# A transformer block and a gated cross-attention: all sixteen heads' probabilities turned by VectorE in 23 of 48 items, with a second exchange through DRAM issued from ScalarE's queue

## The chip, the cores and the metric

One core of one Trainium2 chip. The metric is the device time of one execution in microseconds, the median of three runs. Matrix products run on TensorE (PE), the rest on VectorE (DVE), ScalarE (ACT) and GpSimd (POOL); SyncE (SP) only issues DMAs.

## The reference, cut to what matters

```python
def attention(q, k, v, mask):                       # 16 heads of 32
    scores = einsum('bhqd,bhkd->bhqk', q, k) / sqrt(32)
    scores = scores * mask - 10000.0 * (1.0 - mask)
    return einsum('bhqk,bhkd->bhqd', softmax(scores), v)
# x: (16, 128, 512), enc: (16, 128, 512), float32
y = layernorm(x) @ w_qkv + b_qkv;  x = x + attention(q, k, v of y, mask_a) @ w_ao + b_ao
q = layernorm(x) @ w_q + b_q; k, v = enc @ w_kv + b_kv
x = x + attention(q, k, v, mask_b) @ w_co + b_co
x = x + gelu(layernorm(x) @ w1 + b1) @ w2 + b2
a = layernorm(enc); Q = x @ Wq.T; K, V = a @ Wk.T, a @ Wv.T
out = x + tanh(gate) * (softmax(Q K.T * scale, masked) V) @ Wo.T
```

## The kernel before, in words

There are three attention phases of 16 batch elements (128 tokens each): A (self attention), B (cross attention), then a feed-forward stage, then D (the gated cross attention). An *item* g is one batch element of one phase: g = 0 to 15 in A, 16 to 31 in B, 32 to 47 in D. Every product with a weight is made of three matmuls, hi·hi, hi·lo and lo·hi, of a rounded "hi" part and its remainder "lo" of each float32 operand. Projections are cut in *half units* of 512 PSUM columns per partition, three for each step (`units[0]`, `units[1]`, `units[2]`).

Each engine runs an instruction stream that is written out by hand, and steps of the five streams meet only at semaphores. Step g holds parts of three items:

- **TensorE** (`step`): `times_v(g-2)`, `scores(g)`, the projection of unit 0, `row_sums(g-1)` (a small transpose of the inverse row sums), `transpose_prob(g-1, 2)` and `(g-1, 3)` (four 128x128 transposes each, heads 8 to 15), unit 1, unit 2, `project_out(g-2)`; then the next step's `times_v(g-1)`.
- **ScalarE** (`step`): `context_hi(g-2)`, the copy of the transposed row sums (`row_sums_out`), the copy of unit 0, the copy of the transposed probabilities (`probs_out`, L1194), a weight chunk's hi part, the copy of unit 1, in some steps `fill_scale` or `fill_hi` (the layer norm's scale and bias, or the hi part, on the next pair's inputs), then 16 exponentials (`exps`, L1217; four heads are a quarter).
- **VectorE** (`step`): `context(g-2)` (the division by the row sums), in D the first half of `mask_scores(g)`, `inverse_sums(g-1)` (L1611, after all exponentials of g-1), `context_lo(g-2)` twice (L1633), `mask_scores(g)` (L1590), `row_max(g)` (L1603), in some steps `turn_inputs` (L1535), statistics and hi parts, `turn_blocks(g)` (L1617), and the residual.
- **GpSimd** (`step`): in A and B `add_mask_bias(g)` twice (L2023), between VectorE's masking and its maximum; lo parts of inputs and weights; a bias row on the residual.
- **SyncE** (`step`): all DMAs, in a fixed order.

The probabilities must be turned (keys on partitions) before `times_v`. In the items of `BY_PE` (0, 27 to 32, 44 to 47) TensorE transposes all sixteen heads. In the 37 others it transposes heads 8 to 15, and heads 0 to 7 go another way: the exponentials write them into `prob_blocks`, VectorE turns the 32x32 blocks (`turn_blocks`, one instruction), SP stores the 512 KB tile to DRAM (`store_blocks`, L516) and brings it back with four DMAs of 128 KB, one for each group of 32 partitions, with the blocks in their places (`bring_blocks`, L525). `times_v(g)` waits for the copies by ScalarE and for all four DMAs (`s_moved`). PSUM banks 4 and 5 (`T_BANK`) hold the transposes and the result of `times_v`, banks 6 and 7 (`U_BANK`) the units and the row sums.

Phase A's steps 4, 6, 8, 10 and 14 contain a `fill_scale`, step 13 a `fill_hi` of inputs that need no turning. In D the odd steps to 43 contain a `fill_scale`, the even ones to 44 a `fill_hi`, both after `turn_inputs`.

Of the kernel before, what the change touches and what calls it, by code (L numbers as in the profile page):

```python
# [152 lines left out]

def moved_number(g):

    return g + 1 - sum(k <= g for k in BY_PE)


def transposed_count(g, c):

    return sum(4 if k in BY_PE else 2 for k in range(g)) + (c + 1 if g in BY_PE else c - 1)


def copied_by_act(g, half):

    return sum(2 if k in BY_PE else 1 for k in range(g)) + (half + 1 if g in BY_PE else 1)
# [75 lines left out]
def build(nc, x, first_x, enc, encT, mask_a, mask_b, mask_d, weights, columns, rows, gate, ident_in, out):  # L242
# [3 lines left out]
    with ExitStack() as ctx:  # L246
# [18 lines left out]
        hidden_parts = sb("hidden_parts", [128, 2, 512], f32r)  # L265
        chi = [ctx_parts[:, 0, :], hidden_parts[:, 0, :]]
# [30 lines left out]
        turned = nc.dram_tensor("prob_turned", (2, 128, NH // 2 * T), f32, kind="Internal").ap()  # L297
        spread = nc.dram_tensor("row_sums_spread", (4, KC * T), f32, kind="Internal").ap()
# [20 lines left out]
        s_moved = sem("prob_blocks_moved")  # L319

# [41 lines left out]
        s_turned = sem("prob_blocks_turned")  # L362
        s_clo = sem("ctx_lo")
# [26 lines left out]
        def row_sum_bank(g):  # L390
            return U_BANK if sums_late(g) else U_BANK + 1
# [316 lines left out]
        def pe_program():  # L708
# [105 lines left out]

            def times_v(g):

                phase, q, gp, half = g // 16, (g % 16) // 2, (g // 2) % 2, g % 2
                pe.wait_ge(s_pta, copied_by_act(g, 1))
                if g in BY_PE:
                    pe.wait_ge(s_ptd, copied_by_dve(g, 1))  # L820
                else:
                    pe.wait_ge(s_moved, 64 * moved_number(g))
                if phase == D:
                    pe.wait_ge(s_va, 2 * q + half + 1)
                else:
                    pe.wait_ge(s_v, 16 * phase + 2 * q + half + 1)
                for c in range(KC):
                    for j in range(4):
                        h = 4 * c + j
                        out = ps[32 * j:32 * j + 32, T_BANK + c // 2, T * c:T * c + T]  # L830
                        P = prob[:, g % 2, T * h:T * h + T]
                        if h < NH // 2 and g not in BY_PE:
                            P = by_head(prob[:, g % 2, 0:NH // 2 * T])[:, h]
# [121 lines left out]
            def step(i, st):  # L955
# [19 lines left out]
                if st.prev:  # L975
                    row_sums(g - 1)
                    if g - 1 in BY_PE:
                        transpose_prob(g - 1, 0)
                        transpose_prob(g - 1, 1)
                    else:  # L980
                        transpose_prob(g - 1, 2)
                        if g != 44:
                            transpose_prob(g - 1, 3)
                if not late:
                    if st.prev:
                        row_sums_out(g - 1)
                    project(*st.units[1], U_BANK + 1)
                if g == 44:
                    transpose_prob(g - 1, 3)
# [158 lines left out]
        def act_program():  # L1148
# [53 lines left out]
            def exps(g, quarter, part=None):  # L1202
# [7 lines left out]
                if moved and quarter == 0 and moved_number(g) > 1:  # L1210
                    act.wait_ge(s_pst, 16 * (moved_number(g) - 1))
                for s in range(4 * quarter + (2 if part == 1 else 0), 4 * quarter + (2 if part == 0 else 4)):
                    src = P[:, T * s:T * s + T]
                    dst = src
                    if moved:
                        dst, src = by_head(pblocks[:, :])[:, s], src.rearrange("p (j k) -> p j k", k=32)
# [93 lines left out]
            def step(st):  # L1310
# [25 lines left out]
                if g == 44:  # L1336
# [9 lines left out]
                if not st.ends:  # L1346
                    half_out(*st.units[2])
                if g != 28:
# [157 lines left out]
        def dve_program():  # L1506
# [111 lines left out]

            def prob_out(g, c):
# [88 lines left out]
            def step(st):  # L1708
# [20 lines left out]
                if late:  # L1729
# [254 lines left out]
        def pool_program():  # L1984
# [30 lines left out]

            def add_mask_bias(g, h):
# [170 lines left out]
```

## Time and profile before

| | |
|---|---|
| median of 3 runs | 1102.0 us (1101.92 to 1104.04) |
| profiled execution, span from first to last instruction | 1100.7 us |
| its own time beyond the span | not recorded; 1.3 us lie between the span and the median |
| steps 3 to 14 (71.9 to 250.0 us) | 178.1 us, 12 steps |
| steps 34 to 44 (894.5 to 1053.9 us) | 159.4 us, 11 steps |

A step is counted here from the start of its `scores` (L776) to the start of the next step's. The engines' busy shares say who works; which of them bounds a step is seen from who waits last in it.

### The profile page before, as it was taken

What the parts mean: (1) busy time and instruction counts of PE and PEld (TensorE: products, weight loads), DVE (VectorE), ACT (ScalarE), POOL (GpSimd) and SP (SyncE); (2) the same over time, 40 slices, a digit from 0 to 9 for tenths busy, and PEclk for the clock granted to TensorE, in tenths of its full rate; (3) what the DMA queues carried; (4) which work ended last, traced back from release to release, by engine and by line L of the source; (5) the groups of instructions that cost most, each with busy time, mean ns of one, the idle gap of its engine ahead of it and who ended that gap; (6) DMA issues with size and microseconds to landing.
All of it is one profiled execution on the core that took longest, in us unless ns stands there. A gap on an engine that the chain in (4) does not pass through costs nothing.

```text
span 1100.7 us, 24328 instructions
## 1 busy us (share of the span) xinstructions
PE 1074.7 (98%) x8829; PEld 934.2 (85%) x8829; DVE 815.4 (74%) x1314; ACT 712.7 (65%) x2365; POOL 462.0 (42%) x337
## 2 busy tenths in 40 slices
PE   7989999999999999998999999999999999999998
PEld 6888888888888888886898888888888988888886
DVE  6678787778888778888877557656677478778777
ACT  4678777777788778786444434434444387777776
POOL 3665666557767776767512121103012331122100
PEclk9999999999999999999999999999999999999999
DMA  6366565576776777553241130220622146666633
GB/s 216 98 201 198 191 195 188 174 227 216 221 227 215 223 211 229 180 191 128 85 134 40 38 96 12 85 96 1 181 101 83 59 146 205 203 198 210 177 97 97
DMA packets 136135, 167.04 MB, mean 152 GB/s; under 512 B 16992, under 2 KB 82256, under 8 KB 136016
## 3 DMA queue, kind: packets, MB, share of 16 engines
q1 hardware_dynamic: 136016, 165.50, 47.9%
q8 instruction: 70, 1.15, 0.4%
q14 instruction: 49, 0.40, 0.1%
HBM read 113.15 MB, written 52.29 MB: 150 GB/s over the span
## 4 chain that ended last, share of the span: by engine, by line
PE 59%; DVE 12%; ACT 9%; POOL 7%; issue 4%; DMA 3%; SPq 1%; DVEq 0%; ACTq 0%; POOLq 0%
PE psum L938 15%; PE psum L919 14%; PE psum L758 13%; POOL prob L2023 6%; PE psum L858 5%; PE psum L750 5%; ACT prob L1217 4%; ACT prob_blocks L1217 2%; PE psum L794 2%; PE psum L776 2%; DVE prob L1590 2%; DVE ln_tile L1528 2%; PE psum L835 2%; DVE negmax L1603 2%; ACT inputs_transposed L1255 2%
## 5 line engine op out<-in xcount | busy, mean ns | idle before, releaser
L758 PE MATMUL psum<-inputs_hi,weights_hi 128*128 128x256 f32 x768 | 223.7, 291 | 5.4 <-POOL inputs_lo L2014 2.5
L758 PE MATMUL psum<-inputs_lo,weights_hi 128*128 128x256 f32 x768 | 217.1, 283 | 0.0
L758 PE MATMUL psum<-inputs_hi,weights_lo 128*128 128x256 f32 x768 | 217.0, 283 | 0.0
L2014 POOL TENSOR_TENSOR inputs_lo<-inputs_transposed,inputs_hi 128x512 fp32r<-128x512 f32 x84 | 113.0, 1367 | 228.9 <-DVE inputs_hi L1563 168.4
L2023 POOL TENSOR_TENSOR prob<-prob,mask_bias 128x1024 f32<-128x1024 f32 x64 | 152.7, 2408 | 98.3 <-DVE prob L1590 96.3
L1217 ACT ACTIVATE prob<-prob,negmax 128x128 f32<-128x128 f32 x472 | 182.2, 391 | 0.5 <-DVE negmax L1603 0.5
L758 PEld LDWEIGHTS psum<-inputs_hi,weights_hi 128*128 128x128 f32 x768 | 146.7, 191 | 10.3 <-issue 2.8
L1603 DVE TENSOR_REDUCE negmax<-prob 128x8 f32<-128x1024 f32 x96 | 115.9, 1210 | 50.0 <-POOL prob L2023 50.0
L758 PEld LDWEIGHTS psum<-inputs_lo,weights_hi 128*128 128x128 f32 x768 | 147.0, 191 | 0.2
L758 PEld LDWEIGHTS psum<-inputs_hi,weights_lo 128*128 128x128 f32 x768 | 146.9, 191 | 0.0
L858 PE MATMUL psum<-weights_hi,context_parts 128*128 128x512 f32 x376 | 125.8, 393 | 0.4 <-ACT kT L1168 0.3
L1217 ACT ACTIVATE prob_blocks<-prob,negmax 128x128 f32<-128x128 f32 x296 | 114.4, 389 | 16.9 <-DVE negmax L1603 16.9
L1303 ACT ACTIVATE qT<-psum,columns 128x512 f32<-128x512 f32 (+1 forms) x80 | 46.2, 598 | 106.2 <-PE psum L919 106.2
L1687 DVE SCALAR_TENSOR_TENSOR kT<-kT,qT 128x512 f32<-128x512 f32 x64 | 46.9, 733 | 80.3 <-ACT kT L1308 80.2
L2026 POOL TENSOR_TENSOR residual<-residual,bias_rows 128x512 f32<-128x512 f32 x42 | 57.7, 1378 | 83.3 <-DMA residual<-stream 63.3
L1217 ACT ACTIVATION_READ_ACCUMULATOR prob<-prob,negmax 128x1 f32 x472 | 90.3, 191 | 0.0
L938 PE MATMUL psum<-weights_hi,hidden_parts 128*128 128x512 f32 x264 | 87.7, 392 | 1.1 <-DVE hidden_parts L1682 1.0
L1255 ACT ACTIVATE inputs_transposed<-inputs_transposed,columns 128x256 f32<-128x256 f32 x120 | 62.3, 591 | 37.2 <-DVE inputs_transposed L1535 37.0
L1989 POOL TENSOR_TENSOR weights_lo<-weights_whole,weights_hi 128x512 fp32r<-128x512 f32 x56 | 75.8, 1367 | 21.3 <-ACT weights_hi L1154 21.3
L858 PEld LDWEIGHTS psum<-weights_hi,context_parts 128*128 128x128 f32 x376 | 70.6, 188 | 16.5 <-ACT qT L1303 0.6
L938 PE MATMUL psum<-weights_hi,context_parts 128*128 128x512 f32 x248 | 81.8, 390 | 0.9 <-DVE context_parts L1682 0.9
L1590 DVE SCALAR_TENSOR_TENSOR prob<-psum,mask 128x512 f32<-128x512 f32 x128 | 79.2, 680 | 0.0
(124 smaller groups left out, 2600.3 us busy)
## 6 DMA issues: line engine op xcount, KB each, us to landing
prob_turned<-prob_blocks SPq DMA_DIRECT2D x37, 512.0 KB, 3.0
prob<-prob_turned SPq DMA_DIRECT2D x148, 128.0 KB, 3.3
weights_whole<-weights_in SPq DMA_DIRECT2D x72, 256.0 KB, 3.4
normalised<-ln_tile SPq DMA_DIRECT2D x30, 512.0 KB, 2.8
inputs_transposed<-normalised SPq DMA_DIRECT2D x120, 128.0 KB, 2.9
context<-row_sums_spread SPq DMA_DIRECT2D x188, 64.0 KB, 2.1
stream<-residual SPq DMA_DIRECT2D x42, 256.0 KB, 2.7
residual<-stream SPq DMA_DIRECT2D x42, 256.0 KB, 3.7
```

What stands on the lines that cost most here:

```text
L758: mm = pe.matmul(ps[:, bank, GT * part:GT * part + GT], w[:, slot, c, o], a[:, buf, c, :], start=c == 0 and i == 0, stop=c == KC - 1 and i ...
L858: mm = pe.matmul(ps[:, U_BANK + 1, :], a[0][:, cs], w[:, slot, c, :], start=c == 0 and i == 0, stop=c == KC - 1 and i == 2)
L919: mm = pe.matmul(out, w[:, slot, c, o], a, start=c == 0 and i == 0, stop=c == KC - 1 and i == 2)
L938: mm = pe.matmul(ps[:, accumulator(group, t), :], a[gb][:, tok], w[:, slot, (j * chunks + e) % 4, :], start=j == 0 and e == 0 and i == 0, ...
L1217: ins = act.activation(dst, src, ACT.Exp, bias=negmax[:, par, s:s + 1], accum_out=total[:, par, s:s + 1])
L1255: ins = act.activation(dst, src, ACT.Identity, bias=cols[:, b0 + c:b0 + c + 1], scale=cols[:, g0 + c:g0 + c + 1])
L1590: ins = dve.scalar_tensor_tensor(heads(P[:, 512 * c:512 * c + 512]), ps[:, S_BANK:S_BANK + 4, T * c:T * c + T], SCALE, other.unsqueeze(1). ...
L1603: dve.tensor_reduce(negmax[:, par, 8 * h:8 * h + 8], heads(prob[:, par, 1024 * h:1024 * h + 1024]), AX.X, ALU.max, negate=True).then_inc(s ...
L1989: pool.tensor_tensor(wlo[:, slot, c, :], raw[:, slot, c, :], whi[:, slot, c, :].bitcast(f32), ALU.subtract).then_inc(s_wlo, 1)
L2014: pool.tensor_tensor(lo, y, hi.bitcast(f32), ALU.subtract).then_inc(s_rlo if fill.ln is None else s_flo, 1)
L2023: pool.tensor_tensor(half, half, mb.unsqueeze(1).to_broadcast([128, 8, T]), ALU.add).then_inc(s_biased, 1)
L2026: pool.tensor_tensor(tile, tile, brow[:, ROW_SLOT[name], :], ALU.add).then_inc(s_resb, 1)
```

## The change

Items 2 to 13 and 33 to 43 (`WHOLE`, 23 items) have none of their heads transposed by TensorE. Heads 8 to 15 are written by the exponentials into a new tile, `second_prob_blocks`, turned by a second VectorE instruction right after `inverse_sums(g-1)` in the next step, stored and brought back by one and four DMAs that ScalarE's stream issues: the store after the copy of unit 0, the four loads right before the next exponentials. The eight transposes and ScalarE's copy of 1024 columns go. `times_v` waits for the second exchange (`s_moved2`) and for the row sums' copy. The row sums of these items go to bank 5, after `context(g-1)`, and unit 1 then waits for the residual of g-3 and no longer for that copy. For items 1 to 13 and 32 to 43 the two `context_lo` move from VectorE to GpSimd, at the head of its step.

```diff
+WHOLE = tuple((*range(2, 14), *range(33, 44)))
+LO_BY_POOL = tuple((*range(1, 14), *range(32, 44)))
...
         def row_sum_bank(g):
-            return U_BANK if sums_late(g) else U_BANK + 1
+            return T_BANK + 1 if g in WHOLE else U_BANK if sums_late(g) else U_BANK + 1
...
# TensorE
             def row_sums(g):
                 pe.wait_ge(s_rt, g + 1)
-                if sums_late(g):
+                if g in WHOLE:
+                    pe.wait_ge(s_cx, 2 * g)
+                elif sums_late(g):
...
             def times_v(g):
-                pe.wait_ge(s_pta, copied_by_act(g, 1))
+                if g in WHOLE:
+                    pe.wait_ge(s_rc, g + 1)
+                    pe.wait_ge(s_moved2, 64 * second_number(g))
+                else:
+                    pe.wait_ge(s_pta, copied_by_act(g, 1))
...
-                    else:
+                    elif g - 1 not in WHOLE:
                         transpose_prob(g - 1, 2)
                         if g != 44:
                             transpose_prob(g - 1, 3)
                 if not late:
-                    if st.prev:
+                    if g - 1 in WHOLE:
+                        u_bank_free(g)
+                    elif st.prev:
                         row_sums_out(g - 1)
                     project(*st.units[1], U_BANK + 1)
...
# ScalarE
+            def store_second_blocks(g):
+                n = second_number(g)
+                act.wait_ge(s_turned2, n)
+                if n > 2:
+                    act.wait_ge(s_moved2, 64 * (n - 2))
+                act.dma_start(turned_second[n % 2], second_blocks[:, :]).then_inc(s_pst2, 16)
+
+            def bring_second_blocks(g):
+                n = second_number(g)
+                act.wait_ge(s_pst2, 16 * n)
+                blocks = turned_second[n % 2].rearrange("(i k) (j n) -> j k i n", i=4, j=4)
+                for j in range(4):
+                    dst = prob[32 * j:32 * j + 32, g % 2, NH // 2 * T:].rearrange("p (i n) -> p i n", i=4)
+                    act.dma_start(dst, blocks[j]).then_inc(s_moved2, 16)
...
-                elif st.prev and g != 44:
+                elif st.prev and g != 44 and g - 1 not in WHOLE:
                     probs_out(g - 1)
+                if g - 1 in WHOLE:
+                    store_second_blocks(g - 1)
...
                 if not st.ends:
                     half_out(*st.units[2])
+                if g - 1 in WHOLE:
+                    bring_second_blocks(g - 1)
                 if g != 28:
                     exps(g, 0)
                 exps(g, 1)
...
# VectorE
+            def turn_second_blocks(g):
+                dve.wait_ge(s_exp, 4 * g + 4)
+                dve.transpose(second_blocks[:, :], second_blocks[:, :]).then_inc(s_turned2, 1)
...
                 if st.ends and not late:
                     inverse_sums(g - 1)
+                if g - 1 in WHOLE:
+                    turn_second_blocks(g - 1)
+                if st.ends and not late and g - 2 not in LO_BY_POOL:
                     context_lo(g - 2, 0)
                     context_lo(g - 2, 1)
...
# GpSimd
             def step(st):
+                if g - 2 in LO_BY_POOL:
+                    context_lo(g - 2, 0)
+                    context_lo(g - 2, 1)
                 if phase != D:
                     add_mask_bias(g, 0)
                     add_mask_bias(g, 1)
```

## Rows read from the trace of the kernel before

**Rows 1.** The page: span, and busy us (share) xinstructions of each engine.
```profile
span 1100.7 us, 24328 instructions
PE 1074.7 (98%) x8829; PEld 934.2 (85%) x8829; DVE 815.4 (74%) x1314; ACT 712.7 (65%) x2365; POOL 462.0 (42%) x337
```
**Rows 2.** Stretches: length, busy (x) PE, PEld, DVE, ACT, POOL; clock, DMA share, GB/s.
```profile
71.90:250.00 178.10, 175.20 (x1732) 154.39 (x1728) 137.17 (x215) 134.45 (x527) 108.96 (x72) 1.00 0.61 193
894.50:1053.90 159.40, 157.76 (x1587) 139.67 (x1583) 123.15 (x214) 120.33 (x455) 34.90 (x33) 1.00 0.63 194
```
**Rows 3.** Timeline of PE, step 10: start, length, line, out<-in, count.
```profile
177.12 0.39 PE L776 MATMUL psum<-kT,qT 32*128 32x128 f32 x4
...
181.21 0.27 PE L810 MATMUL psum<-identity,rtotal 128*16 128x128 f32 x1
181.31 1.03 PE L794 MATMUL psum<-identity,prob 128*128 128x128 f32 x8
182.11 0.36 PE L758 MATMUL psum<-inputs_hi,weights_hi 128*128 128x256 f32 x1
...
190.77 1.08 PE L835 MATMUL psum<-prob,v 128*32 128x128 f32 x32
```
**Rows 4.** Timeline of DVE, step 10 and the start of step 12.
```profile
179.76 0.23 DVE L1611 RECIPROCAL rtotal<-total 128x16 f32<-128x16 f32 x1
179.98 0.76 DVE L1633 TENSOR_TENSOR context_parts<-context,context_parts 128x256 fp32r<-128x256 f32 x2
180.66 2.48 DVE L1590 SCALAR_TENSOR_TENSOR prob<-psum,mask 128x512 f32<-128x512 f32 x4
...
208.20 0.26 DVE L1611 RECIPROCAL rtotal<-total 128x16 f32<-128x16 f32 x1 [0.60 <-ACT prob L1217]
```
**Rows 5.** Timeline of ACT, step 10: unit 0 and fill_scale.
```profile
181.69 0.81 ACT L1172 ACTIVATE qT<-psum,columns 128x256 f32<-128x256 f32 x2
186.87 2.08 ACT L1255 ACTIVATE inputs_transposed<-inputs_transposed,columns 128x256 f32<-128x256 f32 x4 [0.77 <-DVE inputs_transposed L1535]
```
**Rows 6.** PE's wait in step 3, which starts at 71.92.
```profile
77.69 0.28 PE L810 MATMUL psum<-identity,rtotal 128*16 128x128 f32 x1 [0.24 <-DVE rtotal L1611]
```
**Rows 7.** SP's issues of the first exchange in step 11.
```profile
195.98 1.76 SPq L525 DMA_DIRECT2D prob<-prob_turned  x4
```
**Rows 8.** L525, the 148 loads of 128 KB: us from issue to landing.
```profile
DMA to landing us min/median/max: 2.5/3.3/4.9
```
**Rows 9.** L516, the 37 stores of 512 KB, the same.
```profile
DMA to landing us min/median/max: 2.6/3.0/5.5
```
**Rows 10.** The page, DMA queues: packets, MB, share of 16 engines.
```profile
q1 hardware_dynamic: 136016, 165.50, 47.9%
```
**Rows 11.** Timeline of DVE in D, step 39 (from 968.72).
```profile
971.37 0.24 DVE L1611 RECIPROCAL rtotal<-total 128x16 f32<-128x16 f32 x1
974.57 1.25 DVE L1535 STREAM_TRANSPOSE inputs_transposed<-inputs_transposed 128x1024 f32<-128x1024 f32 x1
```
**Rows 12.** Timeline of ACT in D, steps 38 (from 954.22) and 39.
```profile
962.84 1.15 ACT L1278 ACTIVATE inputs_hi<-inputs_transposed 128x512 fp32r<-128x512 f32 x2
977.26 2.07 ACT L1255 ACTIVATE inputs_transposed<-inputs_transposed,columns 128x256 f32<-128x256 f32 x4
979.23 0.39 ACT L1217 ACTIVATE prob_blocks<-prob,negmax 128x128 f32<-128x128 f32 x1
985.88 0.71 ACT L1241 ACTIVATE context_parts<-context 128x256 fp32r<-128x256 f32 x2
```
**Rows 13.** Timeline of PE: step 44 begins, and ends.
```profile
1041.46 0.39 PE L776 MATMUL psum<-kT,qT 32*128 32x128 f32 x4
1053.94 0.39 PE L776 MATMUL psum<-kT,qT 32*128 32x128 f32 x4
```
**Rows 14.** Timeline of POOL, step 10.
```profile
182.02 4.77 POOL L2023 TENSOR_TENSOR prob<-prob,mask_bias 128x1024 f32<-128x1024 f32 x2 [5.92 <-DVE prob L1590]
```
**Rows 15.** The page's groups: GpSimd's lo part of 512 columns: busy, mean ns.
```profile
L2014 POOL TENSOR_TENSOR inputs_lo<-inputs_transposed,inputs_hi 128x512 fp32r<-128x512 f32 x84 | 113.0, 1367 | 228.9 <-DVE inputs_hi L1563 168.4
```

More of the change, by code:

```diff
@@ L151, with second_number, turned_by_pe @@
 BY_PE = (0, 27, 28, 29, 30, 31, 32, 44, 45, 46, 47)
+WHOLE = tuple((*range(2, 14), *range(33, 44)))
+LO_BY_POOL = tuple((*range(1, 14), *range(32, 44)))
 def moved_number(g):
     return g + 1 - sum(k <= g for k in BY_PE)
+def second_number(g):
+    return sum(k <= g for k in WHOLE)
+def turned_by_pe(k):
+    return 4 if k in BY_PE else 0 if k in WHOLE else 2
 def transposed_count(g, c):
-    return sum(4 if k in BY_PE else 2 for k in range(g)) + (c + 1 if g in BY_PE else c - 1)
+    return sum(turned_by_pe(k) for k in range(g)) + (c + 1 if g in BY_PE else c - 1)
 def copied_by_act(g, half):
-    return sum(2 if k in BY_PE else 1 for k in range(g)) + (half + 1 if g in BY_PE else 1)
+    return sum(turned_by_pe(k) // 2 for k in range(g)) + (half + 1 if g in BY_PE else 1)
 def copied_by_dve(g, half):
@@ L297, in build @@
         turned = nc.dram_tensor("prob_turned", (2, 128, NH // 2 * T), f32, kind="Internal").ap()
+        turned_second = nc.dram_tensor("second_prob_turned", (2, 128, NH // 2 * T), f32, kind="Internal").ap()
         spread = nc.dram_tensor("row_sums_spread", (4, KC * T), f32, kind="Internal").ap()
@@ L319, in build @@
         s_moved = sem("prob_blocks_moved")
+        s_pst2 = sem("second_prob_blocks_stored")
+        s_moved2 = sem("second_prob_blocks_moved")
         s_scores = sem("scores")
@@ L362, in build @@
         s_turned = sem("prob_blocks_turned")
+        s_turned2 = sem("second_prob_blocks_turned")
         s_clo = sem("ctx_lo")
@@ L831, in times_v @@
                         P = prob[:, g % 2, T * h:T * h + T]
-                        if h < NH // 2 and g not in BY_PE:
-                            P = by_head(prob[:, g % 2, 0:NH // 2 * T])[:, h]
+                        if (h < NH // 2 and g not in BY_PE) or g in WHOLE:
+                            eight = h // 8 * NH // 2 * T
+                            P = by_head(prob[:, g % 2, eight:eight + NH // 2 * T])[:, h % 8]
                             out = out.rearrange("p (i q) -> p i q", q=32)
@@ L984, in step @@
                 if not late:
-                    if st.prev:
+                    if g - 1 in WHOLE:
+                        u_bank_free(g)
+                    elif st.prev:
                         row_sums_out(g - 1)
                     project(*st.units[1], U_BANK + 1)
-                if g == 44:
+                if g == 44 and g - 1 not in WHOLE:
                     transpose_prob(g - 1, 3)
@@ L1211, in exps @@
                     act.wait_ge(s_pst, 16 * (moved_number(g) - 1))
+                second = g in WHOLE and quarter >= 2
+                if second and quarter == 2 and second_number(g) > 1:
+                    act.wait_ge(s_pst2, 16 * (second_number(g) - 1))
                 for s in range(4 * quarter + (2 if part == 1 else 0), 4 * quarter + (2 if part == 0 else 4)):
@@ L1214, in exps @@
                     dst = src
-                    if moved:
-                        dst, src = by_head(pblocks[:, :])[:, s], src.rearrange("p (j k) -> p j k", k=32)
+                    if moved or second:
+                        blocks = second_blocks if second else pblocks
+                        dst, src = by_head(blocks[:, :])[:, s % 8], src.rearrange("p (j k) -> p j k", k=32)
                     ins = act.activation(dst, src, ACT.Exp,
@@ L1335, in step @@
                     half_out(*st.units[1])
-                if g == 44:
+                if g == 44 and g - 1 not in WHOLE:
                     probs_out(g - 1)
@@ L1728, in step @@
                 mask_scores(g, 1)
-                if late:
+                if late and g - 2 not in LO_BY_POOL:
                     context_lo(g - 2, 0)
@@ L2014, in fill_lo, with context_lo @@
                     pool.tensor_tensor(lo, y, hi.bitcast(f32), ALU.subtract).then_inc(s_rlo if fill.ln is None else s_flo, 1)
+            def context_lo(g, h):
+                half = slice(256 * h, 256 * h + 256)
+                pool.wait_ge(s_chi, 2 * g + h + 1)
+                pool.tensor_tensor(clo[0][:, half], ctxn[:, half], chi[0][:, half].bitcast(f32), ALU.subtract).then_inc(s_clo, 1)
             def add_mask_bias(g, h):
```

6 lines of the change are left out of this document (added).

## The prediction

> **What bounds the kernel now.** The page comes first: PE is busy 98% of 1100.7 us, the other engines 42 to 74% [rows 1]. The table of stretches says that this holds in the two that the change touches: steps 3 to 14 last 178.1 us with PE idle for 2.9, steps 34 to 44 last 159.4 with PE idle for 1.6, at a full granted clock [rows 2]. So an average step is 14.8 us in A and 14.5 in D, TensorE's own work. The timeline of one step then gives the order in which others must be ready. Step 10 begins at 177.12; the row sums come 4.1 us into it, the eight transposes from 181.31 hold the first matmul of unit 1 back to 182.11, and at 190.77, 13.65 into the step, `times_v(9)` begins [rows 3]. It takes 1.0 to the next scores. Now heads 8 to 15 of item 9 are ready for it about 6 us in, when ScalarE's copy ends; nothing near the end of a step is late. A second limit lies close by: the softmax chain from one item's last exponential to the next one's. From the reciprocal of step 10 to that of step 12, two steps later, there are 28.4 us [rows 4], against 29.4 of PE's work.
>
> **What goes.** The transposes are worth 182.11 - 181.31 = 0.8 us per step on the path [rows 3], 23 times: 18.4 us. That is the whole possible gain, and it leaves 13.9 us for a step in A and 13.7 in D. ScalarE's copy also goes; it is not on the path. The wait of unit 1 for the row sums' copy goes at no gain: the transposes covered it. The new wait in its place, the residual of g-3, is of the previous step and free.
>
> **What is added, and when it is ready.** The chain is new: last exponential of g-1, reciprocal, second turn, store by ScalarE, landing, four loads by ScalarE, landing, `times_v(g-1)` at the step's end. It has to be through 12.8 us into a shortened step.
>
> The second turn: same instruction and shape as the turn of the inputs, 1.25 us [rows 11]. It stands between the reciprocal and the masking in A, where two `context_lo` of together 0.68 stood (179.98 to 180.66) [rows 4]; the chain of softmax gets 0.55 longer.
>
> The store: ScalarE's stream reaches it when unit 0 is copied, 182.50 - 177.12 = 5.4 us into the step [rows 5]; the turn is done by then. No DMA of ScalarE's exists in this trace. SP's 512 KB stores land in 3.0, bounds 2.6 and 5.5 [rows 9]. I take 3.3, since SP's own four loads run just then: landed at 8.7.
>
> The loads: four of SP's issues take 1.76 us [rows 7], 0.44 each, and one of them lands 3.3 after its issue, bounds 2.5 and 4.9 [rows 8]. From the first issue to the last landing that is 1.3 + 3.3 = 4.6, between 3.8 and 6.2. I take 5.4, above the middle, because of the load that comes with them: 165.5 MB took 47.9% of the engines' time [rows 10], so the 1.05 MB that each step gains take 0.479 x 1100.7 / 165.5 x 1.05 = 3.3 us of all sixteen, and the share of 0.61 to 0.63 [rows 2] goes to above 0.8. An issue by ScalarE could cost it anything from nothing to SP's 0.44; I take SP's, the nearest row. The Trainium skill ("DMA: Bandwidth & Descriptors", Issuing engines are not separate DMA queues) says that DMAs of all issuing engines run on the same 16 engines and interleave, and that a second issuer saves only issuing time. By that rule the queue change brings no bandwidth and the 5.4 stands; if ScalarE's queue had capacity of its own, 5.0 would do and the sum would be 9 us lower. No row of this trace decides it.
>
> Where ScalarE reaches the loads is what matters, and it differs:
> - A without `fill_scale` (steps 5, 7, 9, 11, 12, 13): loads at the store's landing, 8.7. Landed at 14.1, plus `times_v` 1.0: a step of 15.1.
> - A with `fill_scale` (4, 6, 8, 10, 14): `fill_scale` waits for VectorE's turn of the inputs, which waits for the maximum, hence for the chain; it ends at 188.95, 11.8 into the step [rows 5]. The second turn adds 0.55; the reciprocal, 2.6 in at step 10 and 1.7 at step 12 [rows 4], comes 0.4 earlier relative to the longer steps. Loads at 12.0, landed at 17.4, a step of 18.4.
> - A, step 3: the row sums come only 5.8 into it [rows 6], so the turn ends at 6.9, the store lands at 10.2, the loads at 15.6: 16.6.
> - D, odd steps: `fill_scale` ends 979.33 - 968.72 = 10.6 into step 39 [rows 12]; it begins after unit 1's copy, which comes 0.8 earlier without transposes (the turn of the inputs, ending 7.1 in plus 0.55, is done by then [rows 11]). Loads at 9.8, landed at 15.2: 16.2.
> - D, even steps: `fill_hi` ends at 963.99, 9.8 into step 38 [rows 12], again 0.8 earlier: loads at 9.0, landed at 14.4: 15.4.
>
> In all of them TensorE, which has everything else of the step behind it, waits in `times_v`, and behind that wait stand the next scores and projections: no other work of PE can fill it. The store is hidden, since the loads wait behind ScalarE's other work in 16 of the 23 steps.
>
> **The sum.** A: 5 x 18.4 + 6 x 15.1 + 16.6 = 199.2, against 178.1: +21.1. D: ten steps took 1041.46 - 894.50 = 147.0, now 5 x 16.2 + 5 x 15.4 = 158.0: +11.0. Step 44 took 12.5 [rows 13], having one unit less, and is now 15.4: +2.9. Together +35.0 on the profiled span of 1100.7, 1135.7. The median of the runs lies 1.3 above the span: 1137.0.
>
> **What I cost at nothing.** `context_lo` on GpSimd: 512 columns take it 1.37 [rows 15], so two halves about 1.4, at the head of its step, where it idles 5.9 until VectorE has masked [rows 14]; uncovered it would be up to 1.4 in each of 23 steps, 32 us, and taken from VectorE it may give 0.7 each on the softmax chain, which is counted. In D GpSimd idles most of the time. ScalarE is held 1.76 by its loads, so the exponentials start later and end at most 7.1 after that; in D they need 985.88 - 979.23 = 6.65 [rows 12], 9.8 + 1.8 + 6.7 = 18.3, which is 2.1 into the next step, where the row sums are wanted at 4.1. The clock: granted in full in both stretches [rows 2], and gaps of up to 4.5 us in a step are new. No row shows such gaps, so what they do to it is a risk that I don't price.
>
> **The rivals.**
> - *The softmax chain sets the step, the landings don't.* If loads land in 3.8, the chain is next: in A 28.4 + 2 x 0.55 + 1.76 = 31.3 for two steps, 187.8 for twelve, +9.7. In D from the reciprocal at 971.37 to the inputs turned at 975.82, 4.45, then 2.07 or 1.15, exponentials 6.65, the turn 0.55 and the loads' issue 1.76 [rows 11, 12]: 15.5 and 14.6, 165.6 for eleven, +6.2. Span 1116.6, time 1118. For it: the short landings among [rows 8]. Against: it takes the quickest of them in every step.
> - *The DMA engines are the limit.* Loads of 6.2 and stores of 4.4: the six `fill_scale`-free steps and step 3 get 1.9 longer than forecast, the other sixteen 0.8: +26, time 1163. For it: the share above 0.8 on average, with peaks where SP's and ScalarE's exchanges meet. Against: they mostly don't meet, SP's loads being issued at 4 to 6 us [rows 7].
> - *The other side, faster: issues from ScalarE cost next to nothing, and all four transfers run at once.* Then 3.3 from first issue to last landing. A: 5 x 16.3, the six at PE's 13.9, step 3 at 16.1 - 0.8 = 15.3: 180.2, +2.1. D: 14.1 and 13.9 by turns, 140.0 for ten, -7.0; step 44 13.3, +0.8. Together -4.1, span 1096.6, time 1098. It decides from the point at which the loads are through 3 us after their first issue in D. For it: nothing here has ScalarE issue. Against: SP's 0.44 for the same descriptors.
> - *The loads are reached early and all is hidden.* That needs them issued by 8 us; 1102.0 - 18.4 = 1083.6. Against: `fill_scale` stands in front of them in the stream itself.
>
> **How the numbers follow.** The forecast, 1137, has 0.60; the chain alone 0.13; the full engines 0.11; the quick issues 0.09; all hidden 0.04; and 0.03 for something that leaves no difference. The range has to hold the chain's 1118 and the full engines' lower part: 1107 to 1163, leaving out the two fast rivals (0.13) and the worst of the slow one. A measurement of this kernel tells about 0.2% from no change: faster 0.13, same 0.03, slower 0.84.
>
> **What would show it.** The changed profile has 184 transposes fewer; PE waits in `times_v` for DMA `prob<-second_prob_turned` by 1 to 4.5 us in nearly every step, most in 4, 6, 8, 10 and 14; PE's busy share falls from 98% to about 94; steps alternate at 18 and 15 in A. DMA issues by ScalarE of about 0.4 us each stand ahead of the exponentials. I am wrong if `times_v` finds the loads landed, or if PE's idle time stands before the row sums instead, which would be the chain.

## The result, and the profile after

The changed kernel takes 1154.7 us (median of 4 runs, 1152.2 to 1156.2), the kernel before 1102.9 (4 runs): a ratio of 1.047, 95% interval 1.045 to 1.049. The forecast was 1137, its range 1107 to 1163. The sign, the range and the place of the loss are as forecast; the size is 18 us short, and the time lies nearer to the 1163 of the rival "the DMA engines are the limit" than to the forecast.

The page of the changed kernel, for [rows 1], [rows 10] and the clock; the landings stand in rows of its DMA view, and L868 is `times_v`'s line:

```profile
span 1154.8 us, 24095 instructions
PE 1076.2 (93%) x8645; PEld 933.4 (81%) x8645; DVE 822.4 (71%) x1287; ACT 692.8 (60%) x2342; POOL 497.4 (43%) x387
...
q1 hardware_dynamic: 136016, 165.50, 46.9%
q10 hardware_dynamic: 16560, 24.12, 7.0%
...
L868 PEld LDWEIGHTS psum<-prob,v 128*32 128x32 f32 x1504 | 41.4, 114 | 68.2 <-issue 68.1
...
prob_turned<-prob_blocks SPq DMA_DIRECT2D x37, 512.0 KB, 3.1
prob<-prob_turned SPq DMA_DIRECT2D x148, 128.0 KB, 3.6
```

There are 184 transposes fewer (8829 - 8645), q10 is the new queue of ScalarE, and TensorE's weight loads stand 68.1 us still in front of `times_v`, where the same row had 16.6 before. "issue" means that the profile names no releaser; the lines that bring the tile show the new part to be the second exchange. Of the stretches that answer to [rows 2] the first is steps 3 to 14, the second steps 34 to 44; the third is step 4 and the last step 38:

```profile
72.20:274.50 202.30, 172.11 (x1636) 150.26 (x1632) 146.11 (x208) 126.85 (x528) 129.06 (x99) 0.96 0.78 233
920.70:1106.90 186.20, 159.41 (x1499) 139.98 (x1495) 126.90 (x205) 112.89 (x457) 49.78 (x55) 0.93 0.77 229
89.40:109.00 19.60, 14.72 (x153) 13.38 (x149) 13.90 (x22) 13.79 (x55) 12.05 (x10) 0.93 0.87 256
990.80:1009.10 18.30, 16.53 (x137) 14.84 (x137) 12.09 (x19) 10.92 (x47) 3.96 (x4) 0.82 0.70 218
```

A's twelve steps take 202.3 (199.2 forecast, 178.1 before), D's eleven 186.2 (173.4 forecast, 159.4 before). The granted clock is no longer 1.00. One step of it, step 4, in the timelines of ScalarE, its issues and TensorE:

```profile
93.93 0.36 ACTq L1266 DMA_DIRECT2D second_prob_turned<-second_prob_blocks  x1
93.98 0.81 ACT L1207 ACTIVATE qT<-psum,columns 128x256 f32<-128x256 f32 x2
...
98.91 0.60 ACT L1309 ACTIVATE inputs_transposed<-inputs_transposed,columns 128x256 f32<-128x256 f32 x1 [1.40 <-DVE inputs_transposed L1593]
98.92 0.80 ACTq L1274 DMA_DIRECT2D prob<-second_prob_turned  x2
...
100.23 0.45 ACTq L1274 DMA_DIRECT2D prob<-second_prob_turned  x1
100.41 0.59 ACT L1309 ACTIVATE inputs_transposed<-inputs_transposed,columns 128x256 f32<-128x256 f32 x1
```
```profile
93.50 0.27 PE L831 MATMUL psum<-identity,rtotal 128*16 128x128 f32 x1
...
107.15 1.94 PE L868 MATMUL psum<-prob,v 128*32 128x128 f32 x32 [4.88 <-issue]
109.01 2.09 PE L795 MATMUL psum<-kT,qT 32*128 32x128 f32 x32
...
114.96 0.27 PE L831 MATMUL psum<-identity,rtotal 128*16 128x128 f32 x1
```

The store is issued 4.5 us into the step, the loads at 9.5 to 11.3; TensorE waits 4.88 for them. Then its granted clock is at half (1.2 GHz, not 2.4): the 32 score matmuls of step 5 take 2.09 where those of step 6 (125.71) take 1.17, and the next row sums, and with them the next store, come at 5.95 into the step instead of 4.08.

### The profile page after: what moved, and what is told of

Its sections match the earlier page's. It is cut to its first block, busy times and chain, and to the rows that moved or that the text cites. A ratio compares the mean times of both kernels' runs of the same rounds, so it can differ in the third digit from the quotient of the medians.

```text
span 1154.8 us, 24095 instructions
## 1 busy us (share of the span) xinstructions
PE 1076.2 (93%) x8645; PEld 933.4 (81%) x8645; DVE 822.4 (71%) x1287; ACT 692.8 (60%) x2342; POOL 497.4 (43%) x387
## 4 chain that ended last, share of the span: by engine, by line
PE 57%; ACT 11%; DVE 10%; issue 7%; POOL 5%; DMA 5%; SPq 1%; ACTq 1%; DVEq 0%; POOLq 0%
PE psum L971 14%; PE psum L952 14%; PE psum L777 13%; PE psum L891 5%; PE psum L769 5%; POOL prob L2094 5%; ACT prob L1256 3%; ACT prob_blocks L1256 3%; PE psum L795 3%; PE psum L868 2%; DMA normalised<-ln_tile 2%; ACT inputs_transposed L1309 2%; DVE ln_tile L1586 2%; DVE prob L1648 2%; DVE negmax L1661 2%
## 5 line engine op out<-in xcount | busy, mean ns | idle before, releaser
L777 PE MATMUL psum<-inputs_hi,weights_hi 128*128 128x256 f32 x768 | 227.2, 296 | 4.5 <-POOL inputs_lo L2080 2.5
L777 PE MATMUL psum<-inputs_lo,weights_hi 128*128 128x256 f32 x768 | 220.0, 286 | 0.0
L777 PE MATMUL psum<-inputs_hi,weights_lo 128*128 128x256 f32 x768 | 219.7, 286 | 0.0
L777 PEld LDWEIGHTS psum<-inputs_hi,weights_hi 128*128 128x128 f32 x768 | 150.0, 195 | 11.1 <-issue 5.6
L777 PEld LDWEIGHTS psum<-inputs_lo,weights_hi 128*128 128x128 f32 x768 | 150.2, 196 | 0.2
L777 PEld LDWEIGHTS psum<-inputs_hi,weights_lo 128*128 128x128 f32 x768 | 149.9, 195 | 0.0
L1256 ACT ACTIVATE prob<-prob,negmax 128x128 f32<-128x128 f32 x288 | 111.2, 390 | 2.4 <-issue 1.9
L868 PE MATMUL psum<-prob,v 128*32 128x128 f32 x1504 | 54.4, 288 | 50.8 <-issue 46.9
L868 PEld LDWEIGHTS psum<-prob,v 128*32 128x32 f32 x1504 | 41.4, 114 | 68.2 <-issue 68.1
L891 PEld LDWEIGHTS psum<-weights_hi,context_parts 128*128 128x128 f32 x376 | 70.7, 188 | 18.4 <-DVE v L1709 2.0
```

The lines of the kernel that those rows point to most:

```text
L777: mm = pe.matmul(ps[:, bank, GT * part:GT * part + GT], w[:, slot, c, o], a[:, buf, c, :], start=c == 0 and i == 0, stop=c == KC - 1 and i ...
L891: mm = pe.matmul(ps[:, U_BANK + 1, :], a[0][:, cs], w[:, slot, c, :], start=c == 0 and i == 0, stop=c == KC - 1 and i == 2)
L1256: ins = act.activation(dst, src, ACT.Exp, bias=negmax[:, par, s:s + 1], accum_out=total[:, par, s:s + 1])
```

## The experiments

All are timed against the kernel before on the same chip; they are edits of the changed kernel. Behind each ratio to the kernel before stands its 95% interval. Versions that were not timed together are best compared by these ratios, whose intervals tell about 5 us apart.

**1. GpSimd's part alone, and the exchange taken away.**

```diff
 # lo_by_pool_only
-WHOLE = tuple((*range(2, 14), *range(33, 44)))
+WHOLE = ()
```


> Only the context's low parts are on GpSimd (items 1 to 13 and 32 to 43); WHOLE is empty, so the transposes and one exchange stay as before. Theory (the two landings of the new exchange cost the time): this part costs nothing, 1102 +- 2; by the chain of waits in steps 3 to 11 of before, where TensorE waits 0.3 to 1.7 us for the row sums, the 0.68 us taken from VectorE could give up to 3 us back: 1099. Rival (the low parts come late from GpSimd and hold project_out or GpSimd's mask bias): up to 1.4 us in 25 steps, 1115 or more.

1101.3 against 1102.7, ratio 0.999 [0.998, 1.001]: no difference.

```diff
 # no_second_exchange: times_v, step of ScalarE
-                    pe.wait_ge(s_moved2, 64 * second_number(g))
-                    store_second_blocks(g - 1)
-                    bring_second_blocks(g - 1)
 # no_exchange_no_turn: also, in the step of VectorE
-                    turn_second_blocks(g - 1)
```


> The changed kernel without the second exchange: VectorE still turns the second tile, but it is neither stored nor brought back, and times_v does not wait for it, so heads 8 to 15 of the 23 items are left out of the result. Theory (landings): TensorE keeps its 0.8 us in D, 11 steps, and in A as far as the softmax chain (28.4 + 1.1 = 29.5 us for two steps against 27.8 of TensorE) allows: 1102 - 9 to 1102 - 18, so 1084 to 1093, at a full clock throughout. Rival (the second turn and the longer softmax chain cost the time): 1110 or more, with TensorE waiting before the row sums.

> As the run without the second exchange, and VectorE's second turn is left out as well (heads 8 to 15 of the 23 items are neither turned nor multiplied rightly). Theory (TensorE's 0.8 us per step were real, and the second turn's place between the reciprocal and the masking gave them back in A and part of D through the softmax chain): steps of 13.9 in A and 13.7 in D, 1102.6 - 18 = 1084 to 1090. Rival (TensorE's time comes back elsewhere, in the residual wait of unit 1, GpSimd's low parts or the row sums' new bank): 1098 or more.

Without the exchange 1104.4, ratio 1.003 [1.001, 1.005]; without the turn too 1093.5, 0.991 [0.989, 0.994]. Both leave heads 8 to 15 of the 23 items out of the result, and both times lie between what I looked for and the rival. The stretch of steps 3 to 14, of the three kernels in the order above (175.7, 177.4, 169.9 us):

```profile
71.90:247.60 175.70, 174.25 (x1738) 154.72 (x1734) 128.57 (x194) 134.04 (x527) 125.96 (x95) 1.00 0.62 194
```
```profile
71.70:249.10 177.40, 166.44 (x1639) 144.02 (x1635) 140.59 (x201) 122.40 (x508) 123.30 (x94) 1.00 0.62 190
```
```profile
71.80:241.70 169.90, 166.06 (x1636) 143.94 (x1632) 124.55 (x190) 123.42 (x514) 122.53 (x94) 1.00 0.64 199
```

TensorE's busy time fell by 7.8 us (174.25 to 166.44) and the stretch grew by 1.7. Step 5 of the kernel without the exchange, TensorE's timeline:

```profile
101.78 1.17 PE L795 MATMUL psum<-kT,qT 32*128 32x128 f32 x32
...
107.38 0.28 PE L831 MATMUL psum<-identity,rtotal 128*16 128x128 f32 x1 [0.24 <-DVE rtotal L1664]
```

The row sums come 5.6 into it; of steps 4 to 11 the even ones last 13.79, the odd ones 16.15. Their sum of 29.94 is the softmax chain [rows 4], lengthened by the turn: without the turn three of these four pairs take 28.1 to 28.2. So the whole exchange costs about 50 us (1154.7 to 1104.4), and with it free of charge nothing would have been won. In A the chain is the reason. In D steps 34 to 44 took 159.0 without the exchange, hardly less than the 159.4 before; there TensorE waits 4.1 for row sums and 3.2 for copies by ScalarE, and what makes these late was not followed further.

**2. Who issues.** SP issues store and loads, in its fixed order ahead of `spread_row_sums`.

```diff
 # from_sync_queue
+                sp.wait_ge(s_turned2, n)
+                sp.dma_start(turned_second[n % 2], second_blocks[:, :]).then_inc(s_pst2, 16)
...
+                sp.wait_ge(s_pst2, 16 * n)
+                    sp.dma_start(dst, blocks[j]).then_inc(s_moved2, 16)
```


> The second exchange issued by SyncE, store after the first exchange's loads, loads before the spread of the row sums; everything else as changed. Theory (two landings in series, 4.1 and 3.7 us each and about 6 from first load issue to last landing, set the step wherever they are issued): TensorE waits in times_v as long as in the changed kernel, 1145 to 1160. Rival (ScalarE's stream is the place of the loss: 1.8 us of issues before the exponentials, blocked until the store lands, unit copies late): 1125 or less, with TensorE's waits at times_v under 30 us instead of 68.

1149.3, ratio 1.043 [1.041, 1.046]: 5 us better than from ScalarE, if at all, since the two intervals touch. Whose queue carries the whole exchange is about a tenth of the loss. SP's own work behind the exchange then stands still instead, so this does not show that a blocked ScalarE costs nothing (see 5).

**3. The clock.** Sixteen more transposes of the identity before the wait in `times_v` (into a bank that is written over) keep TensorE at work.

```diff
 # keep_tensor_busy: times_v, ahead of its wait
+                    for k in range(16):
+                        pe.transpose(ps[:, T_BANK, 128 * (k % 4):128 * (k % 4) + 128], ident[:, :], ident[:, :])
```


> As changed, with 16 transposes of the identity (1.6 us of TensorE at full clock) in each of the 23 steps before the wait for the second exchange; they go to a PSUM bank that times_v overwrites. Theory (part of the loss is TensorE's clock: it is at 1.2 GHz for 48 us of the changed kernel, which costs up to 24 us of work, and falls after steps with long idle time): the clock is full in most steps and the time falls by 8 to 20 us, to 1135 to 1147. Rival (the lower clock only fills time that the landings would leave idle): 1152 to 1157, no change.

1148.2, ratio 1.043 [1.040, 1.045], between the 1147 that I allowed and the rival's 1152. Both stretches of it, to set beside those of the changed kernel:

```profile
71.90:272.70 200.80, 187.14 (x1832) 167.03 (x1828) 146.49 (x207) 126.27 (x527) 129.31 (x99) 0.99 0.78 235
918.40:1103.30 184.90, 170.93 (x1675) 152.89 (x1671) 130.81 (x204) 113.49 (x459) 50.21 (x55) 0.98 0.80 231
```

The clock's records show 47.8 us at 1.2 GHz in the changed kernel, in 11 pieces, and 17.1 here. The time falls by 6.5: filling the waits removes most of the lower clock, which is thus a consequence of them, and gives little back by itself. In steps 36, 38 and 40 the row sums are back at 4.1 into the step, but D's stretch is only 1.3 shorter: in its odd steps the loads take 6.1 from the first issue to the last landing, against 5.4 in the changed kernel.

**4. Phase D alone, and with the wait of `times_v` taken away.** In the second and third kernel the loads land in a spare tile, so that TensorE doesn't wait for them; the third has SP issue them.

```diff
 # only_in_d, and all that follow but the three quarters
+WHOLE = tuple(range(33, 44))
 # only_in_d_spare_tile
-                    pe.wait_ge(s_moved2, 64 * second_number(g))
-                    dst = prob[32 * j:32 * j + 32, g % 2, NH // 2 * T:]...
+                    dst = raw[32 * j:32 * j + 32, 7, 0:2, :]...
 # d_from_sync_spare_tile: the same, and sp. for act. in store and loads
```


> The changed kernel with WHOLE only in items 33 to 43. Theory (each step pays for itself, landings and clock): D pays what it paid in the changed kernel, 186.2 - 159.4 = 26.8 us, and A and B nothing: 1129 +- 3. Rival (part of D's loss comes from the state in which A and B leave the queues): under 1122.

> As only_in_d, but the four loads of the second exchange land in a spare tile that nobody reads, and times_v does not wait for them (heads 8 to 15 of these items are left out of the result). ScalarE issues the same DMAs at the same place. Theory (TensorE's wait for the second landing is the loss): times_v no longer waits, and what stays is ScalarE's delay of the exponentials, a chain of some 15.0 us per step: 1129 - 20 = 1104 to 1112, clock full. Rival (ScalarE's blocked stream or the load on the DMA engines is the loss): 1120 or more.

> WHOLE only in items 33 to 43; the second exchange is issued by SyncE, its loads land in a spare tile and times_v does not wait for them (heads 8 to 15 of these items are left out of the result). Against only_in_d_spare_tile (same transfers, issued by ScalarE: 1123) it changes only whose stream carries them. Theory (two limits of about the same length lie side by side in D: the two landings before times_v, and ScalarE's stream, blocked until the store has landed and then 1.8 us in issues, which makes the exponentials and the copy of unit 2 late; taking one away leaves the other): with both gone steps of 14.2 as without the exchange, 1100 to 1108. Rival (the load of the transfers on the 16 DMA engines slows everything, whoever issues): 1118 or more.

Ratios: D alone 1127.2, 1.022 [1.019, 1.025]; without TensorE's wait 1123.3, 1.018 [1.015, 1.020]; from SP 1121.5, 1.018 [1.016, 1.021]. The two without TensorE's wait missed the lower times that I looked for. Waits in D with the spare tile, ScalarE issuing (us in total, times, longest):

```profile
ACT prob_blocks L1255 <- issue: 20.7, 10, 3.6
...
PE psum L795 <- ACT qT L1202: 12.0, 5, 3.7
...
PE psum L831 <- DVE rtotal L1671: 8.3, 6, 2.7
```

and with SP issuing:

```profile
PE psum L853 <- DVE rtotal L1671: 20.8, 7, 4.0
...
DVE ln_stats L1580 <- DMA ln_tile<-enc_in: 12.8, 8, 3.9
...
DVE context L1692 <- DMA context<-row_sums_spread: 7.2, 5, 3.0
```

Both leave out the turned values of heads 8 to 15 in D. Each wait that is taken away is replaced. With ScalarE issuing, its exponentials are late; with SP, TensorE waits for the row sums, VectorE being held by transfers that have nothing to do with the exchange, though they share SP's stream with it.

**5. Half as many heads moved.** Heads 8 to 11 alone by VectorE, 256 KB, heads 12 to 15 by TensorE, in A and D. The places move too: the turn stands ahead of the reciprocal, and ScalarE issues the store right after `context_hi` and the loads after the weight split, ahead of the copy of unit 1.

```diff
 # three_quarters
-    return 4 if k in BY_PE else 0 if k in WHOLE else 2
+    return 4 if k in BY_PE else 1 if k in WHOLE else 2
-        second_blocks = sb("second_prob_blocks", [128, NH // 2 * T])
+        second_blocks = sb("second_prob_blocks", [128, NH // 4 * T])
 # three_quarters_from_sync: the same, issued by SP
```


> A version from what was found: in the 23 items VectorE turns twelve heads, not sixteen. Heads 8 to 11 (256 KB) are turned before the reciprocal, stored by ScalarE right after context_hi, about 3.5 us into the step, and brought back after the weight split; heads 12 to 15 are transposed by TensorE and copied by ScalarE as before. Row sums in bank 4. Theory (the landings must be through 12.8 us into the step and the softmax chain must not get longer): loads issued at 7 and landed by 12.5, TensorE saves 0.4 us per step in D and most of A, 1093 to 1099, faster than before. Rival (the landings or the turn still come too late): 1105 to 1125, with waits at times_v.

> As three_quarters (heads 8 to 11 by VectorE, heads 12 to 15 by TensorE), with the 256 KB exchange issued by SyncE: the store ahead of the first exchange's loads, the loads ahead of the spread of the row sums. Theory (in three_quarters ScalarE waits in its own stream for the store to land, 4 to 4.5 us in D, so the exponentials start 14 us into the step instead of 10): without that 1097 to 1106, no slower than before. Rival (256 KB more each way still land too late, or SyncE's stream, blocked on the landing, makes its own work late): 1115 or more.

1131.2, ratio 1.026 [1.023, 1.029], and 1116.1, 1.014 [1.010, 1.017]: no gain, and both missed what I looked for. About half the loss is left from ScalarE with half the bytes, but it does not simply go with the bytes. From ScalarE, A's twelve steps take 179.1 (178.1 before) and D's eleven 186.4, as long as with the whole exchange, at a DMA share of only 0.66. From SP they are 181.4 and 167.2, at 0.73:

```profile
73.40:254.80 181.40, 171.64 (x1687) 151.43 (x1683) 135.50 (x208) 131.77 (x538) 127.46 (x97) 0.98 0.73 224
901.90:1069.10 167.20, 155.50 (x1547) 136.30 (x1543) 124.27 (x204) 117.83 (x470) 50.60 (x55) 0.99 0.73 220
```

A wait of the kernel that issues from ScalarE (us in total, times, longest), all of it in D:

```profile
ACT kT L1204 <- issue: 18.1, 4, 6.1
```

In step 36 this copy of unit 1 starts when the four loads have been issued, and they go out when the store has landed (942.86): ScalarE's stream stands 3.73 us still. So here the blocked stream of ScalarE looks to be most of D's 27 us: the same exchange from SP takes 19 less there.

**6. The load by itself.** In D, ScalarE issues the same store and loads at the same places, but with other data and linked to nothing in the step; then the same with a sixteenth of the bytes.

```diff
 # d_unlinked, against only_in_d_spare_tile
-                act.wait_ge(s_turned2, n)
-                act.dma_start(turned_second[n % 2], second_blocks[:, :])...
+                act.dma_start(turned_second[n % 2], whi[:, 7, 0:2, :]...)...
-                act.wait_ge(s_pst2, 16 * n)
-                blocks = turned_second[n % 2].rearrange(...)
+                blocks = x[0:256, :]...rearrange(...)
 # d_unlinked_small: store [128, 64], each load [32, 64]
```


> Items 33 to 43 only. The same store and four loads as in the changed kernel are issued by ScalarE at the same two places of its stream, with the same sizes and shapes of descriptors, but they carry other data: the store reads a tile of rounded weights, the loads read the input x and land in a spare tile. So nothing waits for the second turn before the store, for the store before the loads, or for the loads before times_v (each only for its own predecessor of a step earlier). The turn on VectorE stays; heads 8 to 15 come into times_v stale, which leaves out their turned values. My theory: what D loses with a spare tile (1123.3, D 182.0) is ScalarE's stream standing still for the store's landing. Then D is at 159 to 164, its value without any exchange (159.0) plus at most 2.2 us of issuing for a step that mostly finds slack, and the time is 1103 to 1109. The rival: the 1.05 MB more per step on the sixteen DMA engines and the five issues of ScalarE are enough to make the transfers that others need late. Then D stays above 172 and the time above 1115.

> As the unlinked run (the same five DMAs of ScalarE in each step of D, at the same places, linked to nothing), but each with a sixteenth of the bytes: the store 32 KB, each load 8 KB. It again leaves out the turned values of heads 8 to 15. The unlinked run took 1122.8 us with D at 182.9, though nothing of the step waited for its DMAs: my theory of ScalarE standing still for the store's landing fell. There the loads of ln_tile from enc landed after 5.4 us (median of 16) where they take 3.7 in the kernel before, and VectorE, the row sums and TensorE waited behind them. My theory now: it is the bytes on the sixteen DMA engines (share 0.79 in that stretch against 0.63 before). Then with small ones D comes back to 159 to 165 and the time to 1102 to 1110, ln_tile's loads landing in 3.1 to 4.0. The rival: the five issues of ScalarE themselves (two of about 0.45 us at a time on its stream, and as many entries among SP's) are what delays the others. Then D stays above 172 and the time above 1114.

Unlinked 1122.8, ratio 1.018 [1.015, 1.020]: D is as long with nothing in ScalarE's stream waiting for the store's landing, so my theory that this alone is D's loss fell. Small 1100.5, 0.999 [0.997, 1.000]: the time came back, and the issues cost nothing that can be measured. The load of the transfers is the cause in this pair; the small ones also have fewer and shorter descriptors, so bytes and descriptors are not told apart. Both leave out the turned values. Steps 34 to 44 of the two:

```profile
893.80:1076.70 182.90, 159.41 (x1499) 139.55 (x1495) 129.71 (x204) 111.75 (x446) 49.91 (x55) 0.93 0.79 232
```
```profile
890.80:1052.00 161.20, 151.55 (x1502) 131.70 (x1498) 131.19 (x204) 110.61 (x441) 50.22 (x55) 0.99 0.65 195
```

Apart from the size of five DMAs in each step the two programs are the same, and they are 21.7 us apart. TensorE's busy time itself differs by 7.9 (159.41 and 151.55), at a granted clock of 0.93 for 0.99. The landing (the last column, median us) of the first kernel, then of the second:

```profile
ln_tile<-enc_in SPq DMA_DIRECT2D x16, 256.0 KB, 5.4
```
```profile
ln_tile<-enc_in SPq DMA_DIRECT2D x16, 256.0 KB, 3.7
```

These medians hold eight loads from ahead of D too. The eight that steps 35 to 41 issue landed after 6.3 on average, 4.7 in the small kernel and 4.2 in the kernel before. Step 38 of the unlinked kernel (from 958.67) on VectorE, then TensorE:

```profile
959.99 0.69 DVE L1579 BATCH_NORM_STATS2 ln_stats<-ln_tile 128x6 f32<-128x512 f32 x1 [4.14 <-DMA ln_tile<-enc_in]
...
966.51 0.24 DVE L1670 RECIPROCAL rtotal<-total 128x16 f32<-128x16 f32 x1
```
```profile
966.82 0.38 PE L831 MATMUL psum<-identity,rtotal 128*16 128x128 f32 x1 [3.92 <-DVE rtotal L1670]
```

A layer norm load of SP's lands late, for two reasons: it was issued 11.0 us into step 37, where the kernel before issues it at 7.0, and the pair took 6.5 and 7.4 to land, against 4.5 and 4.7. VectorE's stream stands 4.14 us still for it, with the turn of the first blocks, the residual, the context and half the masking queued in front of the reciprocal. The exponentials had ended by 961.7; the reciprocal is at 966.5, 7.8 into the step (3.4 in step 38 before, at 957.64), and TensorE waits 3.92. That is a 20.2 us step in which nothing waited for the second exchange.

## Why the prediction was in range, and 18 us short

*TensorE waits in `times_v` for the loads.* Right, in every one of the 23 steps, by 0.8 to 4.9 us: 59.6 of the 68.1 us that the weight loads idle there lie in the two stretches. The 184 transposes and a busy share of 93% came as said. The alternation of 18 and 15 held only at first: steps 4 to 9 in A go 19.6, 16.7, 18.5, 16.2, 17.0, 15.0, and step 10, meant to be a long one, took 14.9.

*What goes, 18.4 us.* Wrong. In the kernel without exchange the 23 steps kept nothing of it (1104.4). In A the softmax chain sets the pair of steps at 29.94; for D the reason stays open. My own rows gave the chain, 28.4 and twice 0.55 for the turn, 29.5 against 29.4 before [rows 4]; I used the chain for one rival and not as a floor under the others, so "all hidden" at 1083.6 and "quick issues" at 1098 could not have come out in A. The sum of the forecast is hardly touched, since its steps were longer than the chain. Two slips in the rivals' sums weigh little: five steps of 15.5 and six of 14.6 are 165.1, not 165.6, and "quick issues" has D's even steps at 13.9 where the text gives TensorE 13.7.

*Where ScalarE reaches the loads.* Wrong in the mechanism. I had them behind the end of `fill_scale` (12.0 into steps 4, 6, 8, 10 and 14) and called the store hidden. They were issued at 9.1 to 10.1 there: in step 4 at 98.92, beside the first of four `fill_scale` that ended at 101.0. In 21 of 23 steps (all but 4 and 34) the first load goes out within 0.03 us of the store's landing, so the store is on the path. The store itself goes out 0.45 behind the row sums, in step 4 ahead of the copy of unit 0 that I had it behind (93.93 and 93.98): 4.4 to 4.6 into the step where the row sums are in time, not 5.4.

*Landings.* Store 4.0 us on average in A, 4.5 in D, against the 3.3 that I took; from the first load's issue to the last landing 6.3 and 5.5, against 5.4. The two misses cancel in part, and that is luck: with `fill_scale` the loads come 2.5 earlier and take 1.2 longer. But for D's loads, the measured landings are closer to those of the rival with the full engines (stores 4.4, loads 6.2) than to mine. By step kind, forecast and measured: A with `fill_scale` 18.4 and 17.6; A without 15.1 and 16.2; step 3 16.6 and 17.2; D odd 16.2 and 16.6; D even 15.4 and 17.5; step 44 15.4 and 16.0. A is 3.1 short in all. Of D's 12.8, the five even steps (34 to 42) make 10.5. In these the row sums come at 5.0 to 7.0 into the step, not at 4.1 as in [rows 3], and so does the store that follows them by 0.45 in ScalarE's stream: 9.7 us late over the five. In step 34 TensorE waits 2.7 for the reciprocal (1.4 before). In the other four the reciprocal has started 3.1 to 3.8 into the step and TensorE does not wait; it is late itself, at half clock at the head of the step. Step 36, from 955.95:

```profile
955.95 1.82 PE L795 MATMUL psum<-kT,qT 32*128 32x128 f32 x32
...
959.36 0.41 PE L777 MATMUL psum<-inputs_lo,weights_hi 128*128 128x256 f32 x1
...
959.88 0.28 PE L777 MATMUL psum<-inputs_lo,weights_hi 128*128 128x256 f32 x1
...
961.55 0.27 PE L831 MATMUL psum<-identity,rtotal 128*16 128x128 f32 x1
```

*The clock, "a risk that I don't price".* It is how those row sums, and with them the store, came late: of the eleven pieces at 1.2 GHz six lie in D's steps, and all but one of the eleven begin in a wait of `times_v` or within 2 us of its end. At half speed 47.8 us of records put up to 23.9 us of work late. Experiment 3 took 30.7 of the 47.8 away and gave back 6.5, so most of this work fell into time that the landings would have left idle.

*The rivals.* Full DMA engines, 0.11 and 1163, was no rival but a cause that acts together with the forecast's. I had the share above 0.8, and it came to 0.77 and 0.78; but I priced the load only in the exchange's own landings, and not in the transfers of SP on which VectorE waits. In D alone it costs 21.7 us without any link (experiment 6, steps 34 to 44), and linking the exchange fully only 3.8 more (186.7 for `only_in_d`). The two do not add: in the changed kernel, where the step is long by the landing wait, VectorE waits 3.9 us for `ln_tile` in these steps, in the unlinked one 15.9. The late `ln_tile` belongs to the unlinked pattern: in the changed kernel and in `only_in_d`, at a share of 0.77, these eight loads landed after 4.6 on average (4.2 before). There the load shows in the landings of the two exchanges. A step of 16.6 comes from the load alone; whether the landing wait alone would make one, no run shows.

*The Trainium skill* ("DMA: Bandwidth & Descriptors", Issuing engines are not separate DMA queues): that a second issuer brings no bandwidth agrees with these runs, 1149.3 from SP and 1154.7 from ScalarE; 5.0 us per exchange, the other value, would have made the sum 9 us lower and the error greater.

*GpSimd's `context_lo`, at nothing.* Right: 1101.3 against 1102.7. A's steps became 2.4 shorter (175.7 for 178.1) in the profile, too little to show in the time.

Left open: whether it is the bytes or the count of their descriptors (a load has 1 KB runs) that fills the engines, and how the 24 us of A and the 27 of D in the changed kernel divide between load, landing wait, ScalarE's stream and clock. Experiment 6 was run for D only, and there the unlinked loads could start before the store had landed, as the linked ones cannot; a linked exchange with few bytes was not run. The span's other 3 us lie in steps 15 to 30, not looked into further. No version here beats the kernel before while it computes all.

## What to carry to other kernels

Before you credit work taken from the busiest engine, work out the next chain with the change in it and hold it under every case as a floor: here it ate what A's steps had to gain. Price an added transfer not only in its own landing but in those of all the others in flight with it: for each, find the first instruction of any engine that waits for it. Test it with the same bytes linked to nothing, and keep in mind that such a test also changes when the transfers meet. An exchange through DRAM is two landings in a row, so look for what starts the first; here it was the row sums, late wherever TensorE came out of a wait at half clock.

## What the runs showed of the hardware

- ScalarE's DMA issues don't wait for the end of the activations ahead of them: loads went out at 98.92 while four `ACTIVATE` ran to 101.0. An issue took 0.45 us (median of 92), like SP's 0.43 (median of 148), the store's 0.35. A wait in front of an issue does hold what stands behind it: in `three_quarters` the copies of unit 1 waited 18.1 us behind the store's landing and the loads' issues.
- 0.98 MB more in each 16.6 us step (share 0.65 to 0.79), linked to nothing, took the landing of an unrelated 256 KB load from 4.7 to 6.3 us (mean of eight), and 21.7 us from eleven steps; the same five issues with a sixteenth of the bytes took nothing. At a share of 0.77, but with the loads issued only after their store had landed, these eight took 4.6.
- Ten of the 23 waits in `times_v`, of 1.9 to 4.9 us, were followed by 3.4 or 6.8 us at 1.2 GHz; waits of 3.15 and 2.23 us (steps 8 and 11) were not. With one stretch more it was 47.8 us in all; scores took 2.09 for 1.17. Small transposes in the gaps cut this to 17.1.
